# A depthwise 7x7 convolution's taps on TensorE: 34 in four column groups over stacked images, instead of 24 as full diagonals

## The reference

```
y = conv(x, dw_w, padding 3, groups = channels) + dw_b      # 49 taps, one weight a channel and tap
y = (y - mean_c(y)) * rsqrt(var_c(y) + 1e-5) * ln_g + ln_b
h = gelu(w1 @ y + b1)
x = x + ls * (w2 @ h + b2)
```

## Time and profile before

| | us |
|---|---|
| median of 3 runs (4356.34 to 4363.23) | 4359.32 |
| the profiled execution's own time | 4359.41 |
| its span, first to last instruction | 4357.7 |
| TensorE matmul busy | 3668.3 (84%) |
| VectorE busy | 3459.3 (79%) |
| ScalarE busy | 2028.2 (47%) |
| POOL busy | 2214.1 (51%) |
| mean granted TensorE clock, share of full | 0.909 |
| layer 2, all four samples (norm scale to next norm's statistics) | 928.3 |

### The profile page before, as it was taken

How to read it: one execution, slowest core, us unless ns; L and a number is a source line. 1 busy time by engine, 2 the same in 40 slices (tenths; PEclk the granted TensorE clock), 3 DMA queues, 4 the chain that set the end, 5 groups by cost and what they waited for, 6 DMA issues and landing times.

```text
span 4357.7 us, 77131 instructions
## 1 busy us (share of the span) xinstructions
PE 3668.3 (84%) x26737; PEld 2295.7 (53%) x26737; DVE 3459.3 (79%) x7009; ACT 2028.2 (47%) x4605; POOL 2214.1 (51%) x2459
## 2 busy tenths in 40 slices
PE   4999789879999969969999968978999977983555
PEld 2666534347777624436777733435777753432444
DVE  5999687579999768759999957858999957764666
ACT  2444432346666542246666742235666653232333
POOL 3444440058878550028878732007887834004775
PEclk9999889889999979979999988989999988986555
DMA  1000100164555300055455400034555510007776
GB/s 46 11 11 11 28 0 0 39 168 147 153 149 156 102 0 1 0 157 151 148 154 151 129 25 1 0 109 140 155 151 153 150 58 0 0 20 198 216 220 176
DMA packets 206470, 401.53 MB, mean 92 GB/s; under 512 B 23090, under 2 KB 121805, under 8 KB 204585
## 3 DMA queue, kind: packets, MB, share of 16 engines
q0 software_dynamic: 92160, 302.06, 23.6%
q1 hardware_dynamic: 113906, 94.92, 7.5%
q10 hardware_dynamic: 54, 0.01, 0.0%
HBM read 337.36 MB, written 59.53 MB: 91 GB/s over the span
## 4 chain that ended last, share of the span: by engine, by line
PE 42%; DVE 26%; issue 11%; POOL 10%; POOLq 4%; DVEq 3%; ACT 2%; DMA 1%; SPq 1%; ACTq 0%
PE bank L657 11%; DVE val L1214 8%; PE bank L519 8%; DVE mxc L1177 6%; DVE xl L1237 4%; POOL G L1578 3%; DVE val L1224 2%; PE bank L683 2%; POOLq L1553 2%; PE bank L699 2%; PE bank L446 2%; PE bank L719 2%; PE bank L542 1%; POOL regq L1578 1%; PE bank L485 1%
## 5 line engine op out<-in xcount | busy, mean ns | idle before, releaser
L1589 POOL TENSOR_TENSOR xl<-pt 128x192 bf16<-128x192 f32 (+1 forms) x1024 | 678.4, 663 | 444.2 <-PE bank L519 216.7
L838 ACT ACTIVATE pt<-bank 128x512 f32<-128x512 f32 x1024 | 608.2, 594 | 575.4 <-PE bank L488 345.7
L1578 POOL DMA_INDIRECT G<-patch_table,idx x576 | 591.6, 1027 | 192.7 <-issue 114.7
L519 PEld LDWEIGHTS bank<-vt,pt 128*128 128x128 bf16 x8192 | 548.7, 98 | 242.6 <-ACT pt L838 3.9
L1177 DVE TENSOR_REDUCE mxc<-bank 128x1 f32<-128x512 f32 x896 | 608.1, 680 | 35.0 <-PE bank L446 33.1
L519 PE MATMUL bank<-vt,pt 128*128 128x129 bf16 (+1 forms) x8192 | 633.2, 220 | 1.1 <-ACT osb L846 1.1
L1237 DVE TENSOR_TENSOR xl<-pt 128x320 bf16<-128x320 f32 (+1 forms) x1024 | 506.0, 495 | 73.2 <-PE bank L519 54.7
L1360 DVE SCALAR_TENSOR_TENSOR G<-xn,vec,G 128x512 f32<-128x512 f32 x736 | 521.9, 749 | 47.2 <-issue 40.7
L1563 POOL TENSOR_TENSOR rs<-ve,mhalf 128x4 f32<-128x4 f32 x32 | 33.7, 1054 | 824.9 <-ACT ve L974 824.9
L519 PE MATMUL bank<-vt,xl 128*128 128x129 bf16 x4096 | 401.4, 221 | 12.1 <-DVE xl L1237 11.8
L657 PE MATMUL bank<-vt,val 128*128 (+1 forms) x1152 | 374.7, 391 | 19.5 <-DVE xl L1152 19.5
(11 more groups left out here) (253 smaller groups left out, 7196.9 us busy)
## 6 DMA issues: line engine op xcount, KB each, us to landing
patch_table<-valt SPq DMA_DIRECT2D x64, 512.0 KB, 6.8
G<-patch_table,idx POOLq DMA_INDIRECT x576
x_cur<-in_x SPq DMA_DIRECT2D x4, 2048.0 KB, 7.6
xl<-in_x SPq DMA_DIRECT2D x32, 256.0 KB
attn_out<-ob SPq DMA_DIRECT2D x32, 256.0 KB, 2.6
x_store<-x_cur SPq DMA_DIRECT2D x4, 2048.0 KB, 6.3
xr<-x_store SPq DMA_DIRECT2D x32, 256.0 KB
out<-fo SPq DMA_DIRECT2D x32, 256.0 KB
```

What stands on the lines that cost most here:

```text
L519: last = mm(O[t // 2][:, c0:c0 + width], image[:, at % ring, t * 128:(t + 1) * 128], vhl[:, values, st, 0:width], start=(st == 0 and part ...
L838: A(pt[:, at % PT_RING, :], ST[at % ST_RING] if n else ST_FIRST[at % 3], ACT.Exp, scale=SCALE).then_inc(s["exp_done"], 1)
L1578: g.indirect_dma_start(out=patches(j, k), out_offset=None, in_=table[:], in_offset=bass.IndirectOffsetOnAxis(ap=idx[:, j * K1 + k:j * K1 + ...
L1589: g.tensor_tensor(pl[:, at % PL_RING, 0:stop], pt[:, at % PT_RING, 0:stop], ph[:, at % PT_RING, 0:stop], ALU.subtract).then_inc(s["pl_p"], 1)
```

## The change

Four images take the place of `xh` and `xl` as TensorE's operands. Image `j` holds channels 32j to 32j+31 four times over its 128 partitions: high, low, high, low. The weights of a tap for group `j` are a 128x32 block of four stacked 32x32 diagonals: high, high, low, low. So four matmuls of 128x32 by 128x512, one for each group and each into its own 32 partitions of the bank, do one tap for all 128 channels, the product of the two low parts included. TensorE gets 34 taps in this form, 12 before the mean, 10 before the variance, 3 before the broadcast and 9 after it. VectorE keeps 15, 7 before the centring and 8 before the scaling, none after it.

The images are made by SyncE: 64 copies a sample, each of 32 partitions and a quarter of the rows, behind `xh_rdy` and `xl_rdy` of their quarter. They lie where `y`, `z` and layer 1's scratch lay (`regk`, `regq`, now one tensor `reg`) and in five slots of `G`; `y` and `z` get two slots each. The weights are built once, by POOL, in 14 portions during steps 48 to 152 of sample 0's attention (every eighth), stored to DRAM, and loaded again in layer 1 of the later samples. ScalarE's diagonals are gone. TensorE's loop over the steps is written out.

```diff
-PE_TAPS = 24
+PE_TAPS = 34
...
+        stacked = [(regb[:, j * HP * HP:(j + 1) * HP * HP] if j < 3 else last_image[:, 0:HP * HP])
+                   .rearrange("p (r w) -> p r w", w=HP) for j in range(4)]
...
+                if dcn:
+                    wait_alone(sp, s["t_ps"], NCH * (n + 1))
+                    sp.dma_start(tapw, tap_store).then_inc(s["tapw_ld"], 16)
+                else:
+                    sp.wait_ge(s["tapw_rdy"], 1)
+                    sp.dma_start(tap_store, tapw).then_inc(s["tapw_out"], 16)
+                    sp.wait_ge(s["tapw_out"], 16)
+                stack_images(n)
...
+            def stack_images(n):
+                edges = (0, PAD + H // 4, PAD + H // 2, PAD + 3 * H // 4, HP)
+                for q in range(4):
+                    part_rows = slice(edges[q], edges[q + 1])
+                    sp.wait_ge(s["xh_rdy"], 8 * n + q + 1)
+                    for part in (0, 2):
+                        for j in range(4):
+                            sp.dma_start(stacked[j][32 * part:32 * part + 32, part_rows, :],
+                                         xh[32 * j:32 * j + 32, part_rows, :]).then_inc(s[f"im{q}"], 16)
+                    sp.wait_ge(s["xl_rdy"], 8 * n + q + 1)
+                    for part in (1, 3):
+                        for j in range(4):
+                            sp.dma_start(stacked[j][32 * part:32 * part + 32, part_rows, :],
+                                         xl[32 * j:32 * j + 32, part_rows, :]).then_inc(s[f"im{q}"], 16)
...
                     def taps(first, stop):
                         for k in range(first, stop):
-                            for part, image in ((0, xh), (0, xl), (1, xh)):
-                                last = mm(as_rows(ST[u][:]), diag(k, part),
-                                          shifted(c, k // 7 - 3, k % 7 - 3, image),
-                                          start=(k == 0 and image is xh and part == 0),
-                                          stop=(k == PE_TAPS - 1 and part == 1))
+                            for j in range(4):
+                                last = mm(as_rows(ST[u][32 * j:32 * j + 32]),
+                                          tapw[:, k * 128 + 32 * j:k * 128 + 32 * j + 32],
+                                          shifted(c, k // 7 - 3, k % 7 - 3, stacked[j]),
+                                          start=(k == 0), stop=(k == PE_TAPS - 1))
...
                         pe.wait_ge(s["y_rdy"], B + 1)
-                        taps(0, 10)
+                        if c % 2 or c == 0:
+                            pe.wait_ge(s[f"im{(c + 1) // 2 if c < NCH - 1 else 3}"], 256 * (n + 1))
+                        taps(0, 12)
...
-                        taps(10, 14)
+                        taps(12, 22)
...
-                        taps(14, 15)
+                        taps(22, 25)
...
-                        taps(15, PE_TAPS).then_inc(s["dwp"], 1)
+                        taps(25, PE_TAPS).then_inc(s["dwp"], 1)
...
-                        A(diag(k, 0), ident[:], ACT.Copy, scale=vec[:, DWW + k:DWW + k + 1])
-                        last = A(diag(k, 1), ident[:], ACT.Copy, scale=dwl[:, k:k + 1])
...
-                        taps(0, 2)
+                        taps(0, 7)
...
-                        taps(2, 12)
+                        taps(7, DVE_TAPS)
...
-                    if conv:
-                        taps(12, DVE_TAPS)
...
+                    op = g.tensor_tensor(tapw[:, first * 128:(first + taps) * 128]
+                                         .rearrange("p (k j e) -> p k j e", j=4, e=32), eye, wgt, ALU.mult)
...
+                    elif at >= 48 and at % 8 == 0 and at // 8 - 6 < 5 + (PE_TAPS + 3) // 4:
+                        tap_weights(at // 8 - 6)
```

More of the change, by code:

```diff
@@ L289, in _ @@
                 sp.dma_start(dst, src).then_inc(s["w_in"], 16)
+            per_group = vecs.rearrange("(j c) v -> c j v", c=32)[:, :, DWW:DWW + PE_TAPS]
+            for part in range(4):
+                sp.dma_start(tap_w[32 * part:32 * part + 32].rearrange("p (j k) -> p j k", k=PE_TAPS), per_group)\
+                    .then_inc(s["tapw_in"], 16)
             tab = table.rearrange("(y x) e -> y x e", x=TW)
@@ L941, in reduced @@
                       scale=isc[32:64, 4:5]).then_inc(s["relu_rdy"], 1)
-                def diagonals(first, stop):
-                    for k in range(first, stop):
-                        A(diag(k, 0), ident[:], ACT.Copy, scale=vec[:, DWW + k:DWW + k + 1])
-                        last = A(diag(k, 1), ident[:], ACT.Copy, scale=dwl[:, k:k + 1])
-                    return last
                 for c in range(4):
@@ L951, in layer1 @@
                 for c in range(NCH):
-                    last = diagonals(PE_TAPS * c // NCH, PE_TAPS * (c + 1) // NCH)
-                    if c == NCH - 1:
-                        last.then_inc(s["diag_rdy"], 1)
                     if c:
@@ L1092, in _ @@
             v.tensor_copy(offwb[:, :, 0:NOFF], offw_s)
-            v.tensor_copy(dwh[:], vec[:, DWW:DWW + KT])
             dve.drain()
@@ L1387, in step @@
                         dve.drain()
-                        v.tensor_tensor(cols(y_all, c), a, b, ALU.add).then_inc(s["y_rdy"], 1)
+                        v.tensor_tensor(y_chunk(u), a, b, ALU.add).then_inc(s["y_rdy"], 1)
                         dve.drain()
@@ L1590, in low_values, with tap_weights @@
                                 ph[:, at % PT_RING, 0:stop], ALU.subtract).then_inc(s["pl_p"], 1)
+            def tap_weights(part):
+                if part == 0:
+                    pool.wait_ge(s["tapw_in"], 64)
+                    g.memset(tap_eye, 0.0)
+                    g.tensor_copy(tap_hi, tap_w)
+                    pool.drain()
+                    g.tensor_tensor(tap_w[64:128], tap_w[64:128], tap_hi[64:128], ALU.subtract)
+                    pool.drain()
+                    g.tensor_copy(tap_w[0:64], tap_hi[0:64])
+                    pool.drain()
+                elif part < 5:
+                    g.affine_select(out=tap_eye, in_=tap_eye, compare_op=ALU.not_equal, fill=1.0,
+                                    base=-32 * (part - 1), pattern=[[-1, 32]], channel_multiplier=1)
+                    pool.drain()
+                else:
+                    first = 4 * (part - 5)
+                    taps = min(4, PE_TAPS - first)
+                    eye = bass.AP(tap_eye.tensor, tap_eye.offset, [tap_eye.ap[0], [0, taps], [0, 4], [1, 32]])
+                    wgt = bass.AP(tap_w.tensor, tap_w.offset + first,
+                                  [tap_w.ap[0], [1, taps], [PE_TAPS, 4], [0, 32]])
+                    op = g.tensor_tensor(tapw[:, first * 128:(first + taps) * 128]
+                                         .rearrange("p (k j e) -> p k j e", j=4, e=32), eye, wgt, ALU.mult)
+                    if first + taps == PE_TAPS:
+                        op.then_inc(s["tapw_rdy"], 1)
             def sampling(n, first, stop):
```

76 lines of the change are left out of this document (37 added, 39 removed).

## The result

The changed kernel takes **4146.08 us**, median of 4 runs (4144.16 to 4148.86), against 4357.83 (4353.37 to 4363.23) for the kernel before on the same chip: a ratio of 0.9515, with a 95% interval of 0.9504 to 0.9527. The forecast was 4118, in a range of 4078 to 4178. The time lies inside the range, 28 us above the point. The profiled execution took 4145.01 us (span 4143.2).

What follows compares the result with a forecast made beforehand. TensorE was taken to bound layer 2's step, with VectorE just under it. Four stages gain 61.4 us each, 246 in all, and 5 is lost in sample 0's attention and setup: 4359 - 246 + 5 = 4118 us, range 4078 to 4178.

Steps and rivals of the forecast that it cites:

- What bounds the kernel: Layer 2's step: TensorE bounds it at 25.42 us, VectorE lies just under, and both must be relieved.
- The column groups: TensorE's taps in layer 2: four grouped matmuls run together, so a tap costs 0.2187 us, as one full matmul.
- Rival 4: Layer 2's taps: the groups do not overlap, a step takes 39.4 us, +108 a sample, 4790 us; chance 0.03.
- The step's switches: TensorE's layer-2 step: four exits at 0.10 and four entries at 0.05, 0.6 us of a 17.7 us step.
- rival 1: Layer 2's steps: every switch of form drains TensorE, 1.3 instead of 0.6 us a step, +18, 4136 us; chance 0.12.
- Five periods: Layer-2 stage, second to seventh mean: five steps each 7.7 us shorter, a gain of 38.6 us.
- VectorE's step: VectorE's part of a layer-2 step, with 15 taps: 16.4 us, beside TensorE's 17.7.
- The start of the stage: Layer-2 stage to its second mean: that mean starts at 658.6 instead of 668.65, a gain of 10.0 us.
- rival 2: Start of the layer-2 stage: the images come late, 7 to 10 us a sample, +28 to 40, about 4152; chance 0.09.
- The eighth mean: End of the layer-2 stage: it follows the seventh mean in 15.0 us instead of 23.7, a gain of 8.7.
- the tail: Layer-2 stage's end: without the idle gap, mean and second MLP layer run at warm prices, a gain of 4.1 us.
- Attention in sample 0: Sample 0's attention: POOL's 14 tap-building portions may hold VectorE, 4 us taken of a bound of 0 to 17.

Runs made afterwards that it cites:

- e4: Changed kernel with 24 stacked taps on TensorE instead of 34, and 25 on VectorE as before the change: 4317.67 us, ratio 0.9913 to the kernel before.
- e5: Changed kernel with 33 taps on TensorE instead of 34 and 16 on VectorE: 4139.68 us, ratio 0.9494 to the kernel before.
- e1: Changed kernel with the fp32 mean and broadcast matmuls written as four column groups: 4132.84 us, ratio 0.9488 to the kernel before.
- e3: Changed kernel with the three taps behind the second MLP layer moved ahead of the variance: 4133.5 us, ratio 0.9484 to the kernel before.
- e2: Changed kernel with all fp32 matmuls of layer 2's steps in column groups, variance and both MLP layers too: 4094.08 us, ratio 0.9398 to the kernel before.
- e6: Changed kernel with VectorE's low parts of the two last quarters computed inside step 0 instead of behind it: 4143.09 us, ratio 0.9504 to the kernel before.
- e8: Changed kernel with POOL issuing the first quarter's eight low-part copies beside SyncE's eight: 4135.65 us, ratio 0.9484 to the kernel before.
- e10: e2 and e6 together, with only two VectorE taps ahead of the centring in step 1: 4085.09 us, ratio 0.9368 to the kernel before.
- e11: e10 with POOL issuing the low copies of the first two quarters: 4068.33 us, ratio 0.9332 to the kernel before.
- e9: Changed kernel with POOL's 14 tap-weight portions all put in the last step of sample 0's attention: 4146.34 us, ratio 0.9509 to the kernel before.
- e7: Changed kernel without low-by-low products, twelve copies a quarter instead of sixteen, matmuls over 96 partitions: 4145.17 us, ratio 0.9508 to the kernel before.

## Why the prediction was right, and where it was off

**What bounds the kernel** held. TensorE is the chain before and after, and e4 and e5 bracket it: with 25 taps on VectorE the step is VectorE's, with 16 it is TensorE's.

**The column groups** held to the digit. A tap of four matmuls costs 0.22 as in the earlier trace rows, with stationary blocks and four images that were new. Rival 4, in which they don't overlap, is out.

**The step's switches** are the first term that failed. The prediction took 0.10 per exit from the earlier trace rows and 0.05 per entry, 0.6 a step, and gave 1.3 as the bound. The step came at 18.35: 7.44 + 9.67 leaves 1.24. So rival 1 was the true case, and its price, four pairs at 0.31 to 0.32, is shown by e1 and e3 in two ways; e2 fits it, once the variance's own gain is taken off. Both halves were taken at about half their price: an exit costs 0.20, not 0.10, and an entry 0.11 or 0.12, not 0.05. What misled was reading the exit from the distance of two starts in the earlier trace rows. The other 0.10 lies in the time of the matmul behind, and those rows have no price for that matmul without an exit ahead of it. The Trainium skill, "TensorEngine Tiling (Array Packing)", section "Key Properties", says that a change of tiling mode drains TensorE. The traces agree: a pair of changes costs 0.31 us. Five periods at 0.65 make 3.3 of the 7.8 us by which the forecast of this stage was too good.

**VectorE's step** at 16.4 held in kind. In the steps between it waits 2.4 us each for TensorE (7.2 in three).

**The start of the stage** is the second term, too good by 3.1, and the copies are the smaller part of that. Issues of SyncE lie 0.63 apart, not the 0.46 of the earlier trace rows, and a copy lands in 2.1, not 2.6: sixteen took 615.8 to 627.4, and the first matmul came 1.8 later behind the norm scale than forecast. The second quarter was expected at 631, 7.4 behind the first, and came at 638.5: 32 issues at 0.63 and the landing make 638.1 from 615.82. So the images were late as rival 2 has it, but not at its price. The second quarter's wait is not in the chain, and of the 1.8 little was left at the broadcast: 0.7 came back in the first taps (9.16 for the 9.9 that the forecast gave them with the lower clock), and 0.6 between variance and broadcast (2.8 for 3.4). The broadcast starts 37.5 us behind the scale, where the forecast had 37.2.

The other 2.8 lie between the broadcast and the second mean: 13.0 us, for the 0.9 + 2.0 + 4.2 + 3.1 = 10.2 of the forecast. The broadcast takes 2.07, the nine taps 3.04, the first MLP layer 5.2 with its wait for the Gelu. For the first 3.7 us the granted clock is 0.50, the lower level, behind waits of TensorE of 2.0 and 1.5 us (`Windows` of after; the third number from the end is the clock):

```profile
650.58:654.30 3.72, 3.72 (x22) 1.13 (x26) 1.95 (x3) 0.00 (x0) 0.00 (x0) 0.50 0.54 134
```

The prediction charged the lower clock to the first taps and put it at nothing here. The trace of before has it in the same place (chain of waits), where a warm step has 0.86 and 5.91:

```profile
647.08 2.07 PE bank L691 x2
649.16 7.97 PE bank L657 x27
```

So this is the failed term of the start: broadcast, taps and first MLP layer of step 1 at warm prices. It is also why e6 gave so little: of the 1.7 us that its sample 0 had won at the broadcast, 0.9 were left at the second mean.

**The eighth mean** held within 0.5, **the tail** within 0.9. The gap ahead of the mean went, and the mean is back at 1.02, but the second MLP layer still takes 5.25 where a warm step has 3.54. It took 3.68 in all stages of e3, in three of e5 and in one each of e4, e6 and e8, and 3.64 as groups in all of e2, e10 and e11; with 3.68 a stage ends 1.7 us sooner behind its eighth mean. In after the granted clock is 0.68 in that piece, in e3 1.00. What decides it was not found, and comparisons of a few us between these kernels carry it along.

**Attention in sample 0** is 2.8 longer, for the 4 that were forecast. Whether POOL's portions cause it stays open, since e9 lies within the scatter.

The sum: the four stages missed by 37 us (246 forecast, 209 measured). That the time still came within 28 us of the forecast is in part luck: some 8 us of small gains elsewhere that the prediction had not counted, and 2 us less than it allowed for the rest, took part of that back.

## What to carry to other kernels

Four column groups turn a 128x32 tap of stacked high and low parts into one matmul's time, but each piece in the other form between them costs 0.31 us. Put the neighbours into the same form: here fp32 matmuls split into four groups of 32 columns cost no more than whole ones. After such a change balance the engines anew. Price the matmuls behind every wait at the clock that the trace of before shows there, and compare all samples, not the first alone, before calling a gain lost.

## What the runs showed of the hardware

- An fp32 matmul of 128x128 by 128x512 in four column groups takes 0.86 us, the same as whole (e1, e2).
- Eight small variance matmuls, 0.98 as full ones with the taps ahead at 2.30, and 0.79 in before, where no groups are near, take 0.26 as groups with the taps ahead at 2.17 (e2); by records 30 of the 32 are in that row.
- Copies of 32 partitions from SBUF to SBUF are issued 0.63 us apart by SyncE, and land 2.1 us after the last issue. POOL issues them 0.56 apart, and its copies land in 2.9 to 3.3 (medians of e8).
- The first taps of a stage run at the lower of the two clocks, 0.43 us apart, and go over to 0.22 at 630.5 us in sample 0 of after, 17.8 behind the norm scale, and at 18.2 to 19.1 in samples 1 to 3. With a first matmul 2.5 us sooner the change came at 17.6 to 18.7 in sample 0 of e8, samples 0 to 2 of e7 and samples 0 and 2 of e11, so the earlier taps all ran at the lower clock. It came at 14.7 to 15.3 in the other samples of these three runs.
